# A transformer block with attention and expert layers: softmax probabilities normalised before their transposes, values as the stationary operand

## The chip, the cores and the metric

The kernel runs on one core of a Trainium2 chip. The metric is the device time of one execution in microseconds; three runs of the kernel before gave 843.80, 843.96 and 844.66 (median 843.96). A core has a matrix engine (TensorE, PE in the profile; its weight loads are PEld), VectorE (DVE), ScalarE (ACT), GpSimd (POOL) and a queue for DMA issues (SyncE, SP). Each works through its own list in order, and they meet at semaphores.

## The reference

`x` is 64 sequences of 750 rows of 128. Three layers follow one another:

```
h   = conv_patches(x) @ W + b           # patches of 16 rows, stride 8: 93 tokens of 128 per sequence
h  += attention(layernorm(h))           # 8 heads of 64; q, k, v each: 128x512 product, then a causal 3-tap filter
      sim  = q k^T * 64^-0.5 - slope_h * |i - j|, masked above the diagonal
      attn = softmax(sim, over j);  out = (attn v) @ wout^T
h  += expert_layer(layernorm(h))        # 16 experts, top 2; per expert the mean over its tokens of silu(x w1^T),
                                        # times w2, mixed by the two routing weights
```

## The kernel before

Sequences are taken in 16 groups of four. The program is written out by hand as a software pipeline over t = 0 to 20 (`run`, `step(t, u, f)` on each engine), and each t has four steps s = 0 to 3, one sequence in each. In step (t, s) an engine does in a fixed order, as far as the stage flags `f` allow: token products of group t (`f.tok`), the first normalisation and its transposes of group t-1 (`f.norm`), the query, key and value products of group t-2 (`f.proj`, three of twelve blocks in a step, each with its tap filter: `tap2` on ScalarE and `conv` on VectorE), attention of sequence n = 4(t-3)+s (`f.attn`), the second normalisation, gating and ranks of group t-4 (`f.gate`), and the scatter of group t-5's rows to the experts' rows in HBM (`f.scat`). t = 6 to 13 run as a hardware loop. A "full group" below is a t in which all stages are on, or all but the scatter.

Attention of one sequence (93 tokens) crosses two steps. In its own step: the scores into the two banks `psS` (a bias product with the identity in bf16, L516, then 8 head products of depth 64, L521), on VectorE the row maximum (L876) and the subtraction into `shifted` (L879). In the next step: 8 transposes of `shifted` back into `psS` (L452), on ScalarE the exponential into `probT` (L700, two halves), then 8 products into `psO` with `probT[:, h]`, 93 keys by 93 queries, as the stationary operand and the values with a column of ones, 93 by 65, moving (L500). Queries then lie on partitions; column 65 of each head is the softmax denominator. VectorE takes its reciprocal (L867) and multiplies (L870) into `attn`, TensorE turns it back by four transposes (L544), ScalarE copies them to `attnT` (L746), and the output projection follows (L576), which VectorE adds to `resid` (L891). The values themselves come by four transposes (L469) and a copy to `vrow` (L710).

Single buffers set much of the order: `psS` serves scores, then transposed probabilities; `psV` serves the value transposes, the transposes of the result and those of the routing weights; `psO` serves the weighting, the output projection (`psWout`), `psHn`, the gate and the ranks. The split products (L406 to L408) are fp32 products in three fp32r parts; their low parts are made by GpSimd (`low`, L1043, and L1096).

GpSimd's list in a step: the small operations of the normalisations (s = 1 and 2), `low` for the next step's token products, `xnT_lo` (s = 3), two indirect scatters (L1106), which wait in s = 0 for the slots that VectorE's `place` writes. From t = 17 on, when `f.norm` is off, all eight scatters of a group are issued at the head of s = 0. VectorE's list begins step s = 0 with `place` (L931), s = 1 and s = 2 with statistics, s = 3 with `choose`; `route` ends s = 2. On ScalarE `normalise` (L684) comes before `tap2` of block 3s+1 in s = 1 and s = 2.

After t = 20 come tables, the expert tiles (L595 to L617, L768 to L794, L995 to L1015), the second expert layer (L633 to L642) and the mix. The change doesn't touch them.

Of the kernel before, what the change touches and what calls it, by code (L numbers as in the profile page):

```python
# [27 lines left out]
ALU = mybir.AluOpType  # L28
# [29 lines left out]
def build(nc, x, w_tok, b_tok, gamma, beta, wq, wk, wv, cq, ck, cv, w_out, w_gate, w1, w2,  # L58
# [3 lines left out]
    with ctx:  # L62
# [41 lines left out]
        vrow = [sb(f"vrow{u}", [NT, H, DH + 1]) for u in range(2)]  # L104
        rmax = sb("rmax", [NT, 2, 4])
        shifted = sb("shifted", [NT, 2, 4, NT])
        probT = sb("probT", [NT, 2, 4, NT])
        rden = sb("rden", [NT, 2, 4])
        attn = sb("attn", [NT, H * DH])
# [50 lines left out]
        with ExitStack() as phase1:  # L160
# [24 lines left out]
        psTot = psO[:, 0, 264:264 + E]  # L185
# [20 lines left out]
        consts_ready, zeros_ready, taps_ready, bias_cast, vones_ready, rwzero_ready = (  # L206
            sem("consts_ready"), sem("zeros_ready"), sem("taps_ready"), sem("bias_cast"),
            sem("vones_ready"), sem("rwzero_ready"))
# [11 lines left out]
        p_tr, p_evac, pv_mm, den_done, norm_done = (  # L220
            sem("p_tr"), sem("p_evac"), sem("pv_mm"), sem("den_done"), sem("norm_done"))
        a_tr, a_evac, out_mm, res_add = sem("a_tr"), sem("a_evac"), sem("out_mm"), sem("res_add")
# [180 lines left out]
        def _(pe):  # L403
# [38 lines left out]

            def step(t, u, f):
                for s in range(GB):
                    n = (t - 3) * GB + s
                    prev = f.attn and s > 0 or f.last and s == 0
                    if prev:

                        pe.wait_ge(shift_done, n)
                        for a in range(2):  # L450
                            for hh in range(4):
                                mm = nc.tensor.transpose(psS[:NT, a, hh * NT:(hh + 1) * NT], shifted[:, a, hh, :],  # L452
                                                         ident[:NT, :NT])
                            mm.then_inc(p_tr, 1)
                    if f.gate and s == 2:
                        wait(pe, hn_ready, t - 3)
                        wait(pe, norm_done, n - 1 if f.attn else B)
                        for b in range(GB):
                            mm = nc.tensor.transpose(psHn[:, b * NT:(b + 1) * NT], hn[u][:, b, :],
                                                     ident[:NT, :NT])  # L460
                        mm.then_inc(hnT_tr, 1)
                    if f.proj and s == 0:
                        proj(t, u, f, 3 * s)
                    if f.attn:
                        if s == 0:
                            pe.wait_ge(conv_done, (t - 2) * NBLK)
                        wait(pe, a_evac, n - 1)
                        for j in range(QB):
                            mm = nc.tensor.transpose(psV[:NT, j * 128:(j + 1) * 128],  # L469
                                                     qkv[1 - u][:, 2 * QB + j, s, :], ident[:, :])  # L470
                        mm.then_inc(v_tr, 1)
                    if f.proj and s > 0:
                        proj(t, u, f, 3 * s)
# [10 lines left out]
                    if f.tok:  # L484
                        tok_taps(t, s, 0, 1)
                    if prev:

                        pe.wait_ge(p_evac, n * 2)
                        pe.wait_ge(v_evac, n)
                        wait(pe, norm_done, n - 1)  # L490

                        wait(pe, res_add, n - 1)
                        if f.gate and s == 2:
                            wait(pe, hnT_evac, t - 3)
                        if f.gate and s == 3:
                            wait(pe, logit_copy, t - 3)
                        if f.scat and s == 0:
                            wait(pe, pos_done, t - 4)
                        for h in range(H):
                            mm = nc.tensor.matmul(psO[:NT, h // 4, (h % 4) * (DH + 1):(h % 4 + 1) * (DH + 1)],  # L500
                                                  probT[:, h % 2, h // 2, :], vrow[(s + 1) % 2][:, h, :],
                                                  start=True, stop=True)
                        mm.then_inc(pv_mm, 1)
# [6 lines left out]
                    if f.attn:  # L510

                        if s == 0 and isinstance(t, int) and t == 3:
                            pe.wait_ge(bias_cast, 4)
                        wait(pe, p_evac, n * 2)
                        for a in range(2):
                            nc.tensor.matmul(psS[:NT, a, 0:4 * NT], ident16[:NT, :NT], bias[:, a, :],  # L516
                                             start=True, stop=False, skip_group_check=True)
                        for hh in range(4):
                            for a in range(2):
                                lo = 64 * a  # L520
                                mm = nc.tensor.matmul(psS[:NT, a, hh * NT:(hh + 1) * NT],  # L521
                                                      qkv[1 - u][lo:lo + 64, hh, s, :], qkv[1 - u][lo:lo + 64, QB + hh, s, :],
                                                      start=False, stop=True, skip_group_check=True)
                        mm.then_inc(s_mm, 1)

                    if f.proj:
                        proj(t, u, f, 3 * s + 1)
                    if f.tok:
                        tok_taps(t, s, 1, 2)
                    if f.attn and prev:  # L530
                        pe.wait_ge(v_evac, n + 1)
                    if f.scat and s == 0:

                        wait(pe, rw_done, t - 4)
                        wait(pe, a_evac, n - 1 if prev else B)
                        mm = nc.tensor.transpose(psRT, rw[:, :, :].rearrange("p b e -> p (b e)"),
                                                 ident[:NT, :NT])
                        if not prev:
                            mm.then_inc(rwT_tr, 1)
                    if prev:  # L540

                        pe.wait_ge(norm_done, n)
                        for j in range(QB):
                            mm = nc.tensor.transpose(psV[:, j * NT:(j + 1) * NT], attn[:, j * 128:(j + 1) * 128],  # L544
                                                     ident[:NT, :NT])
                        mm.then_inc(a_tr, 1)
# [24 lines left out]
                    if prev:  # L571
                        pe.wait_ge(a_evac, n)
                        if f.gate and s == 3:
                            wait(pe, base_done, t - 3)
# [85 lines left out]
        def _(ac):  # L660
# [31 lines left out]
            def step(t, u, f):  # L692
                for s in range(GB):
                    n = (t - 3) * GB + s
                    prev = f.attn and s > 0 or f.last and s == 0
                    if prev:
                        wait(ac, pv_mm, n - 1)
                        for a in range(2):
                            ac.wait_ge(p_tr, n * 2 - 1 + a)
                            nc.scalar.activation(probT[:, a, :, :].rearrange("p h n -> p (h n)"),  # L700
                                                 psS[:NT, a, 0:4 * NT], ACT.Exp).then_inc(p_evac, 1)
# [471 lines left out]
```

## Time and profile before

| | |
|---|---|
| runs | 843.80, 843.96, 844.66 us |
| profiled execution: time, span | 846.1 us, 844.4 us |
| busy, share of the span | PE 89%, PEld 82%, DVE 73%, ACT 56%, POOL 45% |
| granted TensorE clock, mean | 0.943 |
| first and last bias product (L516) | 78.9 and 651.4 us |

The span runs from the first instruction to the last; the execution's time holds 1.7 us around it. A row of the timeline gives start, length, engine, line, operation, output and inputs; where products of one line follow one another, they are merged and the last column counts them. An fp32 product counts as two matmul instructions, a split product's parts (fp32r) and a transpose as one each. Products overlap in their records, so the time that one takes from the next is read from start to start. In the groups by line the numbers behind the first bar are the busy time in us and the mean of one in ns, behind the second the engine's idle time just before them, with what ended it.

### The profile page before, as it was taken

The page shows a single profiled execution, that of the slowest core. Times are in us where ns is not written, and L with a number is a line of the kernel's source. Part 1 is how long each engine was busy: PE and PEld are TensorE (multiplying, and loading weights), DVE is VectorE, ACT ScalarE, POOL GpSimd, SP SyncE. Part 2 cuts the span into 40 slices and gives each one's busy share as a digit, 9 for nine tenths or more (in the row PEclk, how much of TensorE's full clock was granted, in tenths as well). Part 3 has the DMA queues.
Part 4 walks back from the last instruction along what each step waited for, and adds up shares of the span by engine and source line. Part 5 has one row for each costly group of instructions (what it writes and reads, how often), then busy time and mean ns, then how long its engine had stood idle before and what let it go on. Part 6 is the DMA issues. An engine that isn't in the chain of part 4 may idle for free. (4 is left out here: it accounts for less than half of the span.)

```text
span 844.4 us, 20971 instructions
## 1 busy us (share of the span) xinstructions
PE 752.6 (89%) x6670; PEld 696.4 (82%) x6670; DVE 615.9 (73%) x1621; ACT 468.9 (56%) x1021; POOL 383.3 (45%) x408
## 2 busy tenths in 40 slices
PE   5577999999999999999999999999786318999987
PEld 5466999999999999999999999977675208999983
DVE  2145778888888888888888888899573145888865
ACT  3345566656566665656666566555333107899950
POOL 3442243666556565555656556545241552222200
PEclk9787999999999999999999999999898658999989
DMA  6321123332112112111212211050000022222205
GB/s 190 99 72 46 47 72 117 102 104 64 48 47 66 47 47 65 50 46 46 68 46 50 65 48 48 19 208 20 10 15 6 19 69 73 64 62 62 62 17 145
DMA packets 42246, 53.89 MB, mean 64 GB/s; under 512 B 13651, under 2 KB 28947, under 8 KB 41680
## 3 DMA queue, kind: packets, MB, share of 16 engines
q1 hardware_dynamic: 26304, 37.13, 15.5%
q0 software_dynamic: 13120, 14.05, 6.0%
q10 hardware_dynamic: 2768, 2.00, 0.8%
q8 instruction: 32, 0.52, 0.3%
q14 instruction: 22, 0.18, 0.1%
HBM read 42.69 MB, written 10.26 MB: 63 GB/s over the span
## 5 line engine op out<-in xcount | busy, mean ns | idle before, releaser
L1106 POOL DMA_INDIRECT expert_rows<-hn,slot x128 | 167.7, 1310 | 92.5 <-DVE slot L951 59.9
L1043 POOL TENSOR_TENSOR x_lo<-x_raw,x_hi 128x752 fp32r<-128x752 f32 x64 | 114.9, 1795 | 151.7 <-ACT x_hi L667 151.7
L831 DVE SCALAR_TENSOR_TENSOR qkv<-ps,taps,qkv 128x368 f32<-128x368 f32 x192 | 114.0, 594 | 86.2 <-ACT qkv L675 84.6
L675 ACT ACTIVATE qkv<-ps,taps 128x372 f32<-128x372 f32 x192 | 108.6, 567 | 90.1 <-PE ps L408 89.8
L834 DVE SCALAR_TENSOR_TENSOR qkv<-ps,taps,qkv 128x364 f32<-128x364 f32 x192 | 114.6, 597 | 6.8
L406 PE MATMUL ps<-x_hi,wtok_hi 128*128 128x376 f32 x256 | 95.3, 372 | 11.3 <-DVE wtok_lo L811 9.0
L500 PEld LDWEIGHTS psO<-vrow,probT 93*93 93x93 f32 x1024 | 93.5, 162 | 4.7 <-ACT probT L700 3.2
L500 PE MATMUL psO<-vrow,probT 93*93 93x65 f32 x1024 | 93.9, 245 | 2.0 <-ACT probT L700 1.1
L407 PE MATMUL ps<-x_lo,wtok_hi 128*128 128x376 f32 x256 | 89.1, 348 | 0.0
L408 PE MATMUL ps<-x_hi,wtok_lo 128*128 128x376 f32 x256 | 89.0, 348 | 0.0
L576 PE MATMUL psO<-wout,attnT 128*93 128x128 f32 x512 | 70.6, 283 | 18.6 <-ACT attnT L746 15.8
L998 DVE TENSOR_REDUCE qkv<-qkv 128x512 f32 (+1 forms) x108 | 72.3, 681 | 19.1 <-ACT qkv L771 18.6
L406 PE MATMUL ps<-xnT_hi,wqkv_hi 128*128 128x372 f32 x192 | 78.0, 406 | 9.0 <-DVE qkv L834 5.0
L576 PEld LDWEIGHTS psO<-wout,attnT 128*93 128x93 f32 x512 | 63.8, 167 | 22.4 <-ACT attnT L746 19.8
L700 ACT ACTIVATE probT<-psS 93x372 f32<-93x372 f32 x128 | 54.4, 472 | 47.9 <-PE psS L452 47.6
L312 POOL DMA_DIRECT2D xs<-expert_rows x54 | 29.8, 552 | 82.2 <-PE psS L595 41.3
L407 PE MATMUL ps<-xnT_lo,wqkv_hi 128*128 128x372 f32 x192 | 65.0, 339 | 0.0
L408 PE MATMUL ps<-xnT_hi,wqkv_lo 128*128 128x372 f32 x192 | 65.0, 338 | 0.0
L876 DVE TENSOR_REDUCE rmax<-psS 93x8 f32<-93x744 f32 x64 | 59.2, 926 | 7.0 <-PE psS L521 5.9
L667 ACT ACTIVATE x_hi<-x_raw 128x752 fp32r<-128x752 f32 x64 | 52.7, 823 | 19.1 <-DMA x_raw<-in_x 14.4
L879 DVE TENSOR_TENSOR shifted<-psS,rmax 93x744 f32<-93x744 f32 x64 | 59.4, 929 | 5.2
L521 PEld LDWEIGHTS psS<-qkv 64*93 64x93 f32 x1024 | 47.2, 158 | 18.2 <-issue 18.2
(160 smaller groups left out, 1620.7 us busy)
## 6 DMA issues: line engine op xcount, KB each, us to landing
x_raw<-in_x SPq DMA_DIRECT2D x64, 376.0 KB, 3.2
w1s<-in_w POOLq DMA_DIRECT2D x8, 512.0 KB, 4.9
w<-in_w SPq DMA_DIRECT2D x4, 1024.0 KB, 10.3
xs<-expert_rows SPq DMA_DIRECT2D x54, 64.0 KB, 1.8
xs<-expert_rows POOLq DMA_DIRECT2D x54, 64.0 KB, 2.1
out<-resid SPq DMA_DIRECT2D x16, 160.0 KB, 2.4
expert_rows<-hn,slot POOLq DMA_INDIRECT x128, 3.5
qkv<-in_w_tok ACTq DMA_DIRECT2D x4, 256.0 KB, 6.7
```

What stands on the lines that cost most here:

```text
L406: nc.tensor.matmul(dst, w_hi, x_hi, start=start, stop=False)
L407: nc.tensor.matmul(dst, w_hi, x_lo, start=False, stop=False)
L408: return nc.tensor.matmul(dst, w_lo, x_hi, start=False, stop=stop)
L500: mm = nc.tensor.matmul(psO[:NT, h // 4, (h % 4) * (DH + 1):(h % 4 + 1) * (DH + 1)], probT[:, h % 2, h // 2, :], vrow[(s + 1) % 2][:, h, : ...
L576: mm = nc.tensor.matmul(psWout, attnT[:, j, :], wout[:, j, :], start=(j == 0), stop=(j == QB - 1))
L675: nc.scalar.activation(qkv[u][:, k, :, :], psP[(k + 1) % 2][:, 0:GT].rearrange("p (b n) -> p b n", n=NT), ACT.Copy, scale=taps[:, k, 2:3]) ...
L831: nc.vector.scalar_tensor_tensor(dst[:, :, 1:NT], src[:, :, 0:NT - 1], taps[:, k, 1:2], dst[:, :, 1:NT], ALU.mult, ALU.add).then_inc(tap1_ ...
L834: nc.vector.scalar_tensor_tensor(dst[:, :, 2:NT], src[:, :, 0:NT - 2], taps[:, k, 0:1], dst[:, :, 2:NT], ALU.mult, ALU.add).then_inc(conv_ ...
L879: nc.vector.tensor_tensor(shifted[:, :, :, :], heads(psS, NT), rmax[:, :, :].unsqueeze(3).broadcast_to([NT, 2, 4, NT]), ALU.subtract).then ...
L998: nc.vector.tensor_reduce(part[:, bass.ds(i, 1), :].rearrange("p i j -> p (i j)"), act[k][:, :].rearrange("p (j n) -> p j n", n=128), AXX, ...
L1043: nc.gpsimd.tensor_tensor(x_lo[u][:, 0:PIECE], x_raw[u][:, :], x_hi[u][:, 0:PIECE].bitcast(F32), ALU.subtract)\
L1106: nc.gpsimd.indirect_dma_start(rows, bass.IndirectOffsetOnAxis(slot[1 - u][:, c:c + 1], 0), hn[1 - u][:, c % GB, :], None)\
```

## The change

- The subtraction writes to one of two new buffers `prob` (queries on partitions). ScalarE takes the exponential there, in place, in the same step; VectorE sums each head's row and takes the reciprocal; GpSimd multiplies in place. The transposes then turn finished probabilities, and ScalarE's two copies after them are plain copies.
- `vrow` loses its column of ones. In `weigh` the values (93 by 64) are stationary and `probT` moves (93 by 93); heads alternate between output partitions 0 to 63 and 64 to 127, so that `psO` holds the result already transposed. `attn`, its product, its four transposes and their semaphores go.
- Each engine's order in a step is written anew: the scores open the step on TensorE, the probabilities' transposes come after half of the token products and wait for the current sequence's subtraction; on VectorE maximum and subtraction open the step, and `place` follows the reciprocal; on ScalarE x_hi comes first and `normalise` last.

```diff
+            def scores(t, u, s, n):
+                if s == 0:
+                    wait(pe, conv_done, (t - 3) * NBLK + 2 * QB)
...
+                wait(pe, shift_done, n)
+                wait(pe, p_evac, (n - 1) * 2)
...                                                  (bias and head products as before)
+            def values(t, u, f, s, n):
+                if s == 0:
+                    pe.wait_ge(conv_done, (t - 2) * NBLK)
+                wait(pe, v_evac, n)
+                if f.scat and s == 1:
+                    wait(pe, rwT_evac, t - 4)
...                                                  (four transposes as before)
+            def turn_prob(f, s, n):
+                pe.wait_ge(prob_ready, n)
+                if f.attn:
+                    pe.wait_ge(shift_done, n + 1)
+                for a in range(2):
+                    for hh in range(4):
+                        mm = nc.tensor.transpose(psS[:NT, a, hh * NT:(hh + 1) * NT], prob[(s + 1) % 2][:, a, hh, :],
+                                                 ident[:NT, :NT])
+                    mm.then_inc(p_tr, 1)
+            def weigh(s, n):
+                pe.wait_ge(p_evac, n * 2)
+                pe.wait_ge(v_evac, n)
+                wait(pe, a_evac, n - 1)
+                wait(pe, res_add, n - 1)
+                for hh in range(4):
+                    for a in range(2):
+                        mm = nc.tensor.matmul(psO[64 * a:64 * a + 64, 0, hh * NT:(hh + 1) * NT],
+                                              vrow[(s + 1) % 2][:, 2 * hh + a, :], probT[:, a, hh, :],
+                                              start=True, stop=True)
+                mm.then_inc(pv_mm, 1)
```

The order on TensorE in a step after the change: `scores`, `proj` 3s, `values`, transposes of tokT (s = 0) or xn (s = 3), token taps 0 and 1, `turn_prob`, transposes of hn (s = 2), `proj` 3s+1, tap 2, transpose of rw (s = 0), `weigh`, gate (s = 2) or ranks (s = 3), tap 3, `proj` 3s+2, output projection.

```diff
@@ ScalarE, order in a step: high, tap2 3s, value copy, resid (s = 0), xnT and xnT_hi (s = 3), then
+                    if f.attn:
+                        ac.wait_ge(shift_done, n + 1)
+                        p = prob[s % 2][:, :, :, :].rearrange("p a h n -> p (a h n)")
+                        nc.scalar.activation(p, p, ACT.Exp).then_inc(exp_done, 1)
...                      the two copies to probT (ACT.Copy), hnT (s = 2), tap2 3s+1, rwT (s = 0), attnT from
...                      psO[:, 0, 0:GT] behind pv_mm, egap (s = 3), tap2 3s+2, normalise (s = 1, 2), tokT (s = 3)
@@ VectorE, order in a step: maximum, subtraction into prob, stats (s = 1, 2), choose (s = 3), conv 3s, then
+                    if f.attn:
+                        dve.wait_ge(exp_done, n + 1)
+                        wait(dve, prob_ready, n)
+                        nc.vector.tensor_reduce(den[:, :, :], prob[s % 2][:, :, :, :], AXX, ALU.add).then_inc(sum_done, 1)
+                        dve.wait_ge(sum_done, n + 1)
+                        nc.vector.reciprocal(rden[:, :, :], den[:, :, :]).then_inc(rden_done, 1)
+                    if f.scat and s == 0:
+                        place(t - 5, 1 - u)
...                      conv 3s+1, rank (s = 3), conv 3s+2, residual addition, route (s = 2)
@@ GpSimd, after xnT_lo and before the two scatters of the step
+                    if f.attn:
+                        pool.wait_ge(rden_done, n + 1)
+                        p = prob[s % 2][:, :, :, :]
+                        nc.gpsimd.tensor_tensor(p, p, rden[:, :, :].unsqueeze(3).broadcast_to([NT, 2, 4, NT]), ALU.mult)\
+                            .then_inc(prob_ready, 1)
```

## Rows read from the trace of the kernel before

**Rows 1.** Busy time by stage; columns in order: stage, length, PE, PEld, DVE, ACT, POOL, clock, DMA, GB/s.
```profile
78.91:112.82 33.91, 33.91 (x314) 32.06 (x313) 26.40 (x51) 20.89 (x42) 9.65 (x9) 1.00 0.17 47
112.82:551.76 438.94, 438.94 (x4139) 415.24 (x4139) 372.25 (x1044) 267.09 (x562) 253.82 (x252) 1.00 0.22 62
551.76:583.73 31.97, 29.38 (x296) 25.39 (x295) 29.91 (x87) 18.01 (x41) 14.17 (x18) 1.00 0.30 110
583.73:623.99 40.26, 32.66 (x289) 28.83 (x289) 29.22 (x79) 15.56 (x34) 12.91 (x13) 0.87 0.05 11
623.99:693.90 69.91, 31.45 (x289) 26.43 (x288) 28.96 (x117) 13.66 (x33) 33.14 (x32) 0.71 0.13 32
```

**Rows 2.** TensorE in order of time, within one step of a full group (start, length).
```profile
303.31 1.46 PE L500 MATMUL psO<-vrow,probT 93*93 93x65 f32 x16
304.61 0.48 PE L516 MATMUL psS<-bias,ident 93*93 93x372 bf16 x2
305.02 0.90 PE L521 MATMUL psS<-qkv 64*93 64x93 f32 x16
305.85 0.44 PE L406 MATMUL ps<-xnT_hi,wqkv_hi 128*128 128x372 f32 x1
306.13 0.33 PE L407 MATMUL ps<-xnT_lo,wqkv_hi 128*128 128x372 f32 x1
306.30 0.33 PE L408 MATMUL ps<-xnT_hi,wqkv_lo 128*128 128x372 f32 x1
307.49 0.48 PE L544 MATMUL psV<-ident,attn 93*128 93x93 f32 x4
307.76 0.41 PE L406 MATMUL ps<-x_hi,wtok_hi 128*128 128x376 f32 x1
308.01 0.34 PE L407 MATMUL ps<-x_lo,wtok_hi 128*128 128x376 f32 x1
308.88 1.04 PE L576 MATMUL psO<-wout,attnT 128*93 128x128 f32 x8
```

**Rows 3.** TensorE in order of time, the expert phase's second layer.
```profile
819.26 5.92 PE L639 MATMUL ps<-w,mean 128*32 128x128 f32 x128 [0.36 <-DVE mean L1021]
```

**Rows 4.** Groups by line and shape, whole span (busy us, mean ns, idle before).
```profile
L1043 POOL TENSOR_TENSOR x_lo<-x_raw,x_hi 128x752 fp32r<-128x752 f32 x64 | 114.9, 1795 | 151.7 <-ACT x_hi L667 151.7
L1096 POOL TENSOR_TENSOR xnT_lo<-xnT,xnT_hi 128x372 fp32r<-128x372 f32 x16 | 15.8, 985 | 10.6 <-ACT xnT_hi L726 10.6
L876 DVE TENSOR_REDUCE rmax<-psS 93x8 f32<-93x744 f32 x64 | 59.2, 926 | 7.0 <-PE psS L521 5.9
L879 DVE TENSOR_TENSOR shifted<-psS,rmax 93x744 f32<-93x744 f32 x64 | 59.4, 929 | 5.2
L870 DVE TENSOR_TENSOR attn<-psO,rden 93x512 f32<-93x512 f32 x64 | 43.9, 686 | 3.1 <-DVE rden L867 0.2
L867 DVE RECIPROCAL rden<-psO 93x8 f32<-93x8 f32 x64 | 12.7, 198 | 8.8 <-PE psO L500 8.8
L667 ACT ACTIVATE x_hi<-x_raw 128x752 fp32r<-128x752 f32 x64 | 52.7, 823 | 19.1 <-DMA x_raw<-in_x 14.4 <-PE ps L408 4.7
L675 ACT ACTIVATE qkv<-ps,taps 128x372 f32<-128x372 f32 x192 | 108.6, 567 | 90.1 <-PE ps L408 89.8
L710 ACT ACTIVATE vrow<-psV 93x512 f32<-93x512 f32 x64 | 38.2, 597 | 10.3 <-PE psV L469 10.3
L723 ACT ACTIVATE xnT<-ps,bet,gam 128x372 f32<-128x372 f32 x16 | 10.6, 661 | 23.7 <-PE ps L508 23.7
L726 ACT ACTIVATE xnT_hi<-xnT 128x372 fp32r<-128x372 f32 x16 | 8.2, 513 | 0.5
L700 ACT ACTIVATE probT<-psS 93x372 f32<-93x372 f32 x128 | 54.4, 472 | 47.9 <-PE psS L452 47.6
```

**Rows 5.** GpSimd in order of time, around one late train of scatters.
```profile
622.64 1.37 POOL L1106 DMA_INDIRECT expert_rows<-hn,slot  x1 [24.99 <-DVE slot L951]
635.21 0.19 POOL L1077 TENSOR_SCALAR veps<-mv 93x4 f32<-93x4 f32 x1
```

More of the change, by code:

```diff
@@ L446, in step @@
                     prev = f.attn and s > 0 or f.last and s == 0
[L447 to L462, printed above, removed]
+                    if f.attn:
+                        scores(t, u, s, n)
+                    if f.proj:
                         proj(t, u, f, 3 * s)
                     if f.attn:
[L465 to L473, printed above, removed]
+                        values(t, u, f, s, n)
                     if f.norm and s == 0:
@@ L483, in step @@
                         mm.then_inc(tok_tr, 1)
[L484 to L503, printed above, removed]
                     if f.norm and s == 3:
@@ L509, in step @@
                         mm.then_inc(xnT_tr, 1)
[L510 to L524, printed above, removed]
+                    if f.tok:
+                        tok_taps(t, s, 0, 2)
+                    if prev:
+                        turn_prob(f, s, n)
+                    if f.gate and s == 2:
+                        wait(pe, hn_ready, t - 3)
+                        wait(pe, base_done, t - 4)
+                        for b in range(GB):
+                            mm = nc.tensor.transpose(psHn[:, b * NT:(b + 1) * NT], hn[u][:, b, :],
+                                                     ident[:NT, :NT])
+                        mm.then_inc(hnT_tr, 1)
                     if f.proj:
@@ L572, in step @@
                         pe.wait_ge(a_evac, n)
-                        if f.gate and s == 3:
-                            wait(pe, base_done, t - 3)
                         for j in range(QB):
@@ L695, in step @@
                     prev = f.attn and s > 0 or f.last and s == 0
[L696 to L701, printed above, removed]
-                    if f.gate and s == 2:
-                        wait(ac, hnT_tr, t - 3)
-                        nc.scalar.activation(hnT[:, :], psHn, ACT.Copy).then_inc(hnT_evac, 1)
+                    if f.tok and f.more(t, s):
+                        ac.wait_ge(x_in[(s + 1) % 2], t * (16 * GB // 2) + (16 * ((s + 1) // 2) + 16))
+                        high(t * GB + (s + 1), (s + 1) % 2)
+                    if f.proj:
+                        tap2(t, u, 3 * s)
                     if f.attn:
@@ L752, in step @@
                         tap2(t, u, 3 * s + 2)
+                    if f.norm and s == 2:
+                        normalise(t - 1, rstd, shift, xn, ln_shift, xn_ready)
+                    if f.gate and s == 1:
+                        wait(ac, scattered[u], (t - u - 4) * (16 * GB))
+                        normalise(t - 4, rstd2, shift2, hn[u], ln2_shift, hn_ready)
                     if isinstance(t, int) and t == 0 and s == GB - 1:
@@ L800, in _ @@
         def _(dve):
-            for u in range(2):
-                nc.vector.memset(vrow[u][:, :, DH:DH + 1], 1.0).then_inc(vones_ready, 1)
             nc.vector.memset(zeros[:, :], 0.0).then_inc(zeros_ready, 1)
```

129 lines of the change are left out of this document (60 added, 69 removed).

## The prediction

> **What bounds the kernel now.** I read the page first (busy shares and the forty slices), then cut the span at the first bias product (L516) of a group of four sequences and asked for busy time by stage, then laid out one step's instructions, then the groups by line, then the drain. The reader is to see three things. From 112.8 to 551.8 us, which is twelve groups of four steps, TensorE is busy for all of the 438.9 us, so a group takes 438.94/12 = 36.58 us and nothing but TensorE's own instruction stream sets it; VectorE is busy 372.3 of them (31.0 a group), ScalarE 267.1 (22.3) and GpSimd 253.8 (21.2) [rows 1]. The group before (78.9 to 112.8) is the same kind, so 13 groups are TensorE's. In the next group, without token products, VectorE carries 29.9 of 32.0 us [rows 1]. In the last three groups of attention and gating (583.7 to 693.9) TensorE is busy for little more than half: these are chains of waits, and there the order of operations counts. The expert phase (150.5 us) isn't touched.
>
> **The change on TensorE, full groups.** Removed per step: the weighting with probabilities stationary, from 303.31 to the next line's start at 304.61, 1.30 us; and the four transposes of the normalised result, 307.49 to 307.76, 0.27, after which the first split product takes 0.25 instead of 0.17 to hand over (307.76 to 308.01, against 306.13 to 306.30): 0.35 in all [rows 2]. Added: the weighting with values stationary, 16 instructions of 93 columns that alternate between the lower and the upper 64 output partitions. Nearest row from below: the scores, also 16 instructions of 93 columns in pairs, on two halves of the rows; they take 305.02 to 305.85, 0.83, and cost 0.11 more at the next product (305.85 to 306.13 against 0.17) [rows 2]. That parts of the columns also run side by side is borne out at L639: 128 instructions of 128 columns on four column quarters take 5.92 us [rows 3], where the output projection takes 1.04 us for 8 of that width [rows 2], a pace at which 128 would need 16 us. So eight slots, 0.83 + 0.11, and about 0.10 for entering, which sits in the 0.41 us from the bias products to the first score: 1.03 us (an estimate; ends 0.66, eight slots of 0.083 and no edge, and 1.60, sixteen in a row with both edges). Moving the probability transposes between split products adds one more hand-over, 0.05 to 0.08. Net per step: -1.30 - 0.35 + 1.03 + 0.05 = -0.57, so 36.58 - 2.28 = 34.3 a group.
>
> The Trainium skill ("TensorEngine Tiling (Array Packing)", section "Key Properties") says that a change of tiling mode drains TensorE. By that the kernel now pays twice per step where it paid once; the two edges of the scores (0.11 behind them) are what the trace shows of it. If the drain were free, a step would be 0.2 cheaper than in my sum.
>
> **What is late next.** All other engines get a new chain: scores, row maximum, subtraction, then in the same step the transposes of the probabilities of the sequence before reuse the scores' banks, so they wait for this subtraction. On VectorE that is 0.93 + 0.93 [rows 4] from the scores' end and three hand-overs, 2.1 us (an estimate); TensorE has three projection products, four value transposes and six token products to do meanwhile: 9 x 0.17 [rows 2] + about 0.4 and the edges, 2.1. A tie in steps 1 and 2, with 0.3 to 0.4 to spare in 0 and 3. Any lateness of VectorE now stalls TensorE at once, where before it had a whole half step to spare.
> VectorE's load: the product with the reciprocal (0.69) goes, a sum over 744 elements (by the maximum's row, 0.93) comes, the reciprocal stays [rows 4]: 31.0 + 4 x 0.24 = 32.0 a group, or 32.6 with gaps between; below 34.3, but step 2 alone (statistics and routing) holds about 9.4 against TensorE's 9.
> ScalarE: step 3 starts with the normalisation of step 2 still running (moved to the end of its step), then x_hi 0.82, scaling 0.57, values 0.60, xnT 0.66 and its high part 0.51 come ahead of the exponential (about 0.8, by x_hi's width) and of the two copies (2 x 0.47) [rows 4]. Sum from the scores' end about 5 us; TensorE wants the copies after about 4.2. A stall near 0.5 once a group.
> GpSimd: four products of 744 elements, each about 1.78 by the 752-element row (1.80) [rows 4]: 21.2 + 7.1 = 28.3 busy, and 0.3 of idle issue behind each of 8 scatters, with gaps 33. That fits under 34.3 with little to spare; the product is due only in the next step, so it is covered. Its broadcast operand isn't in the trace; bounds 0.99 (the 372-element row, L1096) and 2.8 (that row on top of L1043's 1.80) [rows 4]; I take the row of like width.
> Of the possible 0.3 to 1 us of stalls I take 0.5, so 34.8 a group: 13 x (36.58 - 34.8) = -23 us.
>
> **The stages behind.** In the group from 551.8 VectorE is nearly full already and gains 1.0 of work: +0.8. In the groups of 583.7 and 624.0 GpSimd issues eight scatters in one train, released by the slots that `place` writes: at 622.64, until its next work at 635.21, 12.6 us [rows 5]; four small operations and ScalarE's normalisation follow, and TensorE waits for it. `place` moves from the head of step 0 behind scores (1.2), maximum and subtraction (2.0), exponential (0.8), sum and reciprocal (1.1): the train starts 5.1 us later. And the product of sequence 0 now stands behind the train in GpSimd's order, and before it those small operations: 1.8 more, on the path to TensorE's transposes, copies and weighting. Walking both groups through their waits gives +7.3 for the second (no projections in it) and +4.1 for the first, where projections and their additions had filled the time anyhow. The group after that has no attention and keeps its train; the start, before 78.9, gets a few reordered ScalarE operations: 0, bounds -1 and +2.
>
> Sum: -23.4 + 0.8 + 4.1 + 7.3 = -11.2. Against the profiled execution's 846.1 us that is 834.9; the median of the runs is 2.1 below that execution, so **832.5 us**.
>
> **Rivals.**
> *The drain and the edges cost nothing (0.15).* Weighting at 0.66 and no stalls: TensorE 33.0 and VectorE 32.6 a group bound alike, about 33.3: 13 x 3.3 = -43, with +12 behind: 813. For it: the eight-slot rhythm of the scores; against it: the 0.11 edge and the tie at the subtraction.
> *VectorE is held by GpSimd (0.15).* `place` sits right behind the reciprocal that releases GpSimd's product. If VectorE's first two-operand instruction there has to wait until that product ends (1.8 [rows 4]), step 0 takes VectorE 9.6 against TensorE's 8.5; the next step's subtraction comes 1.0 to 1.6 late in every group that scatters: +11 to +18 us, 844 to 850, the gain gone. In the trace no such pair has met, so no row tells for or against. The Trainium skill has this as a rule ("SBUF — State Buffer", section "SBUF: two separate sides": an exclusive lock for a whole instruction, between GpSimd and a VectorE operation with two SBUF inputs); this is the rule that speaks against the change.
> *GpSimd becomes the bound (0.08), slower than before.* Place: its in-order stream of casts, products and scatters. From a product of about 2.2 us on (33 + 4 x 0.45 = 34.8) it sets the group; at its upper bound of 2.8 the group is 33 + 4 x 1.0 = 37.0: 13 x 0.4 = +5, with +12 behind: 861. At 2.5, near 848.
> *Column halves don't run side by side (0.05).* Sixteen in a row, 1.60: 0 net per step, stalls 0.2: 36.8 a group, +3, and +12: 859. Against it stands L639.
> *The drain of the pipeline costs twice my walk (0.07):* +24 instead of +12: 845.
> The forecast itself, 818 to 843, has 0.50.
>
> **Numbers.** About 0.2% (1.7 us) is what a measurement of this kernel can tell from no change. Faster: forecast and first rival, 0.65 and a little of the others, 0.68. Same: the lower edge of VectorE's case and of the long drain, 0.07. Slower 0.25. The range takes the first rival's value and VectorE's case whole, and leaves out serial columns and a slow GpSimd: 812 to 853.
>
> **What would show it.** Right: the bias products 34.5 to 35 us apart per group, the weighting's 16 instructions within 0.85 us, TensorE's waits short and on the subtraction or the copies, the first scatter of the last groups 5 us deeper in its step. Wrong: the weighting at 1.3 us or more; GpSimd's product over 2.3 us or GpSimd busy for over 95% of a group; VectorE's `sel` lengthened or late beside a GpSimd product; TensorE idle for 1 us per step.

## The result, and the profile after

The changed kernel takes **899.22 us** (median of 4 runs, 891.68 to 903.10); the kernel before takes 843.88 (842.54 to 844.66) on the same chip. The ratio is 1.0647, with a 95% interval of 1.0574 to 1.0719: **slower**. The forecast was 832.5 us with a range of 812 to 853, so it was wrong in sign and in size. The profiled execution took 900.48 us, with a span of 898.7.

Busy time by stage, cut at the bias product of a group (now L452), with the columns of [rows 1]: the group of t = 3 (nothing to gate yet), twelve full groups, the group without token products (t = 16), the group of t = 17, and the rest up to the last train of scatters. Then two single steps, both a step 0.

```profile
66.83:98.26 31.43, 30.61 (x278) 27.06 (x277) 27.16 (x52) 22.60 (x43) 15.38 (x13) 1.00 0.19 55
98.26:575.88 477.62, 434.75 (x3950) 380.67 (x3949) 406.03 (x1037) 302.38 (x611) 318.94 (x297) 0.96 0.20 55
575.88:615.90 40.02, 32.05 (x284) 27.20 (x283) 33.76 (x89) 22.30 (x47) 21.48 (x22) 0.86 0.31 115
615.90:663.61 47.71, 34.16 (x275) 28.83 (x273) 30.46 (x80) 19.34 (x39) 19.06 (x18) 0.79 0.05 11
663.61:736.67 73.06, 40.02 (x292) 32.77 (x290) 24.48 (x103) 17.09 (x37) 29.59 (x29) 0.57 0.05 12
334.68:347.94 13.26, 10.50 (x82) 9.04 (x81) 10.39 (x24) 6.81 (x13) 9.38 (x7) 0.89 0.16 41
375.15:386.88 11.73, 9.04 (x83) 7.64 (x82) 9.48 (x23) 6.19 (x13) 8.81 (x7) 1.00 0.18 43
```

The reader is to see that a full group takes 477.62/12 = 39.80 us instead of 36.58, that TensorE now stands still for 42.9 us of the twelve groups where it had stood still for none, and that its clock there is no longer 1.00. Added up against [rows 1]: the first bias product comes 12.1 us earlier (66.83 against 78.91), these 13 groups cost 36.2 more (509.05 against 472.85), the group behind them 8.1 more, the next 7.4, and what follows up to the last train of scatters (736.67 against 681.18) 15.9. That makes 55.5; what follows, most of it the expert phase, gives 1.2 back.

From bias product to bias product the four steps of a full group took 8.7, 8.9, 9.55 and 9.5 us. Now they take 11.7 to 13.5, 8.1, 9.1 and 9.85 in most groups. Over the twelve full groups step 0 costs 45.7 us more, step 3 costs 7.3 more, and steps 1 and 2 cost 8.3 and 6.0 less, which is near the forecast. So **nearly all of the loss is in step 0**. Step 0 in order of time (start, length, engine, idle before and its releaser):

```profile
381.10 0.20 DVE L869 RECIPROCAL rden<-den 93x8 f32<-93x8 f32 x1
381.22 0.11 DVE L924 TENSOR_SCALAR wden<-egap 93x4 f32<-93x4 f32 x1
381.38 1.43 POOL L1092 TENSOR_TENSOR prob<-prob,rden 93x744 f32<-93x744 f32 x1 [0.41 <-DVE rden L869]
381.46 1.49 DVE L928 TENSOR_TENSOR sel<-hot,pos 93x128 f32<-93x128 f32 x1
...
383.50 0.22 DVE L944 TENSOR_TENSOR rw<-wsel 93x64 f32<-93x64 f32 x1
...
383.78 0.30 PE L543 MATMUL psV<-ident,rw 93*128 93x93 f32 x1 [2.68 <-DVE rw L944]
384.08 0.87 PE L493 MATMUL psO<-probT,vrow 93*64 93x93 f32 x16
```

TensorE's stream now has the transpose of the routing weights (L543) ahead of the weighting. It waits for `rw`, the last product of `place`, and `place` has gone behind the sum and the reciprocal. The waits of TensorE over ten full groups that scatter (total us, times, longest):

```profile
PE psV L543 <- DVE rw L944: 27.3, 10, 2.9
PE psS L481 <- DVE prob L851: 9.9, 10, 1.0
```

Once per group TensorE waits 2.7 us for `rw`, and once, in step 3, 1.0 us for the subtraction. Within the first wait stands `sel` at 1.49 us; where no GpSimd work runs beside it, it takes 0.26. The second wait comes from `route` at the end of step 2: it holds VectorE from 366.59 to 368.24, and the row maximum of step 3, whose scores ended at 366.62, begins only behind it:

```profile
366.59 0.21 DVE L888 COPY logit<-psO 93x64 f32<-93x64 f32 x1
...
368.10 0.14 DVE L897 TENSOR_TENSOR gap<-top 93x4 f32<-93x4 f32 x1
368.16 0.92 DVE L848 TENSOR_REDUCE rmax<-psS 93x8 f32<-93x744 f32 x1
...
370.19 0.90 PE L481 MATMUL psS<-ident,prob 93*93 93x93 f32 x8 [1.03 <-DVE prob L851]
```

The groups of the new instructions, and `sel` (busy us, mean ns, idle before):

```profile
L1092 POOL TENSOR_TENSOR prob<-prob,rden 93x744 f32<-93x744 f32 x64 | 91.3, 1427 | 88.0 <-DVE rden L869 87.9
L867 DVE TENSOR_REDUCE den<-prob 93x8 f32<-93x744 f32 x64 | 58.6, 915 | 11.5 <-POOL prob L1092 8.9 <-ACT prob L719 2.6
L719 ACT ACTIVATE prob<-prob 93x744 f32<-93x744 f32 x64 | 52.7, 823 | 22.4 <-DVE prob L851 22.4
L928 DVE TENSOR_TENSOR sel<-hot,pos 93x128 f32<-93x128 f32 x16 | 18.7, 1170 | 0.0
```

The weighting in a step 2, which answers to the first line of [rows 2]: its 16 products are through at the next line's start, after 0.79 us.

```profile
361.84 0.87 PE L493 MATMUL psO<-probT,vrow 93*64 93x93 f32 x16
362.63 0.83 PE L551 MATMUL psO<-wgate,hnT 128*93 128x16 f32 x8
```

The clock. Of the two step 0 above one takes 13.26 us and one 11.73 with nearly the same instructions. In the longer one the wait ends at 343.42, TensorE runs on at 0.98 until 345.0, and from there the granted clock is 0.50, the 1.2 GHz level. The clock fell to 0.50 within 2 us of the end of this wait in 8 of the 11 full groups that scatter. The row:

```profile
345.00:346.50 1.50, 1.50 (x7) 1.47 (x6) 0.00 (x0) 0.14 (x2) 1.20 (x2) 0.50 0.09 12
```

In the late groups GpSimd's order is what [rows 5] showed, with the product in it:

```profile
634.78 1.28 POOL L1102 DMA_INDIRECT expert_rows<-hn,slot  x1 [0.30 <-issue]
636.09 1.44 POOL L1092 TENSOR_TENSOR prob<-prob,rden 93x744 f32<-93x744 f32 x1
637.62 0.19 POOL L1068 TENSOR_SCALAR veps<-mv 93x4 f32<-93x4 f32 x1
```
```profile
637.58 1.56 PE L481 MATMUL psS<-ident,prob 93*93 93x93 f32 x8 [7.46 <-POOL prob L1092]
```

The product of sequence 0 stands behind a train of eight scatters (623.64 to 636.06), and TensorE waits 7.46 us for it.

### The profile page after: what moved, and what is told of

Read it like the earlier page. It is cut to its first block and busy times, and to the rows that moved or that the text cites. A ratio compares the mean times of both kernels' runs of the same rounds, so it can differ in the third digit from the quotient of the medians.

```text
span 898.7 us, 20634 instructions
## 1 busy us (share of the span) xinstructions
PE 752.1 (84%) x6414; PEld 659.8 (73%) x6414; DVE 656.0 (73%) x1619; ACT 516.6 (57%) x1085; POOL 475.2 (53%) x472
## 5 line engine op out<-in xcount | busy, mean ns | idle before, releaser
L1092 POOL TENSOR_TENSOR prob<-prob,rden 93x744 f32<-93x744 f32 x64 | 91.3, 1427 | 88.0 <-DVE rden L869 87.9
L406 PE MATMUL ps<-x_hi,wtok_hi 128*128 128x376 f32 x256 | 99.8, 390 | 9.5 <-DVE wtok_lo L805 8.6
L481 PE MATMUL psS<-ident,prob 93*93 93x93 f32 x512 | 58.8, 261 | 40.4 <-DVE prob L851 26.5
L481 PEld LDWEIGHTS psS<-ident,prob 93*93 93x93 f32 x512 | 49.6, 168 | 54.9 <-issue 23.7
L574 PE MATMUL psO<-wout,attnT 128*93 128x128 f32 x512 | 81.7, 313 | 1.8 <-ACT attnT L737 1.7
L574 PEld LDWEIGHTS psO<-wout,attnT 128*93 128x93 f32 x512 | 76.3, 192 | 3.9 <-ACT attnT L737 2.8
L867 DVE TENSOR_REDUCE den<-prob 93x8 f32<-93x744 f32 x64 | 58.6, 915 | 11.5 <-POOL prob L1092 8.9
L457 PEld LDWEIGHTS psS<-qkv 64*93 64x93 f32 x1024 | 51.1, 170 | 21.3 <-issue 21.3
L719 ACT ACTIVATE prob<-prob 93x744 f32<-93x744 f32 x64 | 52.7, 823 | 22.4 <-DVE prob L851 22.4
```

The costliest lines, as they stand in the source:

```text
L406: nc.tensor.matmul(dst, w_hi, x_hi, start=start, stop=False)
L574: mm = nc.tensor.matmul(psWout, attnT[:, j, :], wout[:, j, :], start=(j == 0), stop=(j == QB - 1))
L1092: nc.gpsimd.tensor_tensor(p, p, rden[:, :, :].unsqueeze(3).broadcast_to([NT, 2, 4, NT]), ALU.mult)\
```

## Experiments

Ratios are to the kernel before on the same chip. Unless said otherwise a kernel is the changed one with the edit shown. "Full groups" are measured from bias product to bias product, "the drain" from the last transposes of tokens (L481 before, L515 after) to the start of the last train of scatters, that of t = 20 (131.2 us before, 158.5 after). They are read from the one profiled execution of each kernel; the times are medians of all.

**1. The transpose of the routing weights late in its step.** On TensorE, behind the output projection; ScalarE's copy `rwT` behind the last tap filter. The edit in short:

```diff
 (TensorE, step 0, ahead of `weigh`)
-    wait(pe, rw_done, t - 4); nc.tensor.transpose(psRT, rw, ...)
 (TensorE, step 0, behind the output projection)
+    wait(pe, rw_done, t - 4); nc.tensor.transpose(psRT, rw, ...)
```


> The changed kernel with one thing moved: TensorE's transpose of the routing weights (which waits for VectorE's place) goes from ahead of the weighting to the end of step 0, and ScalarE's copy of it behind the last tap scaling. Theory A (the loss in full groups is this wait, 2.7 us, and the TensorE clock that falls after it): step 0 of a full group goes from 13.3 to about 9.0 us, the group from 40.2 to 36.0, granted clock 1.00 from 147 us on; the whole 845 to 855 us. Theory B (VectorE is the bound, held by GpSimd's products through the shared port, and TensorE's wait only shows it): step 0 stays at 11.5 or more because place still ends at the same time and the next step's subtraction comes late; 880 us or more.

Measured: 857.84 us (856.93 to 858.68), ratio 1.0162 (1.0136 to 1.0188). That is 3 us above theory A's range and far from theory B's 880. The wait is gone, step 0 is 8.9 us, most full groups are 36.6 to 36.9, and TensorE's clock there is 1.00. Taking this one wait out, with its clock loss, brought back **41 of the 55 us**. `sel` still takes 1.5 us, and now it costs something one step later: VectorE ends the list of step 0 late, so step 1's subtraction is late, and TensorE waits 0.7 to 1.0 us for it. Step 1 takes 9.0 us where it was 8.1:

```profile
294.03 0.90 PE L481 MATMUL psS<-ident,prob 93*93 93x93 f32 x8 [0.73 <-DVE prob L851]
```

**2. `place` back at the head of VectorE's step 0.**

```diff
+    if f.scat and s == 0: place(t - 5, 1 - u)     # ahead of the row maximum
...
-    if f.scat and s == 0: place(t - 5, 1 - u)     # behind the reciprocal
```


> The changed kernel with place back at the head of VectorE's step 0, as in the kernel before; the transpose stays ahead of the weighting. Theory A: the wait for the routing weights goes too, but row maximum and subtraction come 1.2 us later in step 0, less 0.4 of slack: step 0 about 9.8 us, group 36.8; and the trains of eight scatters in the last groups start 5 us earlier in their step, so the drain gets shorter by some 8 to 10 us: about 850 us in all, near or a little below the other variant. Theory B (port): place no longer meets GpSimd's product, so sel falls from 1.47 to 0.26 us and the same 850 would follow; the two theories part on the other variant. If the drain's loss was not from place, the drain stays as long as now (158 us from the last transpose of tokT to the last scatter train).

Measured: 898.98 us (895.4 to 899.08), ratio 1.0646 (1.062 to 1.0673): a miss. `place` no longer meets the product, it meets a scatter's issue and GpSimd's low part of x:

```profile
259.43 1.29 POOL L1102 DMA_INDIRECT expert_rows<-hn,slot  x1 [0.30 <-issue]
...
259.91 2.64 DVE L941 CAST slot<-slotf 93x8 int32<-93x8 f32 x1
260.74 1.78 POOL L1033 TENSOR_TENSOR x_lo<-x_raw,x_hi 128x752 fp32r<-128x752 f32 x1
...
264.64 1.26 PE L481 MATMUL psS<-ident,prob 93*93 93x93 f32 x8 [3.84 <-DVE prob L853]
```

A cast of 8 columns takes 2.64 us (0.16 elsewhere) and ends with `x_lo`; the row maximum and the subtraction are late, and TensorE waits 3.84 us. Step 0 takes 14.2. The drain is 16.6 us shorter, as expected.

**3. No product on GpSimd.** The probabilities are not normalised; TensorE waits for the reciprocal instead.

```diff
-    nc.gpsimd.tensor_tensor(p, p, rden[...].broadcast_to(...), ALU.mult).then_inc(prob_ready, 1)
-    pe.wait_ge(prob_ready, n)
+    pe.wait_ge(rden_done, n)
```


> GpSimd's product is left out, so the probabilities are not normalised and the output is not the reference's; TensorE's transposes wait for the reciprocal in its place. Theory A: the 2.7 us wait in step 0 shrinks by sel's 1.2 us only, and with it part of the clock loss: step 0 about 10.5 to 12, group 37.5 to 39, and 1.4 us shorter per late group; about 875 us. Theory B (GpSimd's product is the cause): the group falls to 36 and the whole to 850 or less.

Measured: 885.87 us (884.96 to 886.78), ratio 1.0491 (1.0455 to 1.0527). Neither number. Step 0 falls to 9.9 to 10.1 in most groups, but GpSimd, now earlier, runs `x_lo` beside another small instruction, ahead of step 3's row maximum. TensorE's wait for the subtraction grows from 1.0 to 2.4 us, and step 3 takes 12.7 to 14.3, part of it at the lower clock:

```profile
289.17 1.81 POOL L1032 TENSOR_TENSOR x_lo<-x_raw,x_hi 128x752 fp32r<-128x752 f32 x1
...
289.45 1.56 DVE L896 TENSOR_TENSOR gap<-top 93x4 f32<-93x4 f32 x1
```

`gap` subtracts 4 columns; alone it takes 0.14. So the hold is not a matter of the new product.

**4. The weighting one column half after the other**, so that neighbours share output partitions.

```diff
-    for hh in range(4):
-        for a in range(2):
+    for a in range(2):
+        for hh in range(4):
```


> The weighting takes all heads of the lower 64 output partitions first, then those of the upper, so that neighbouring products share a column half. If the halves ran side by side before, the 16 instructions take about 1.3 us in place of 0.8, 0.5 more per step, 64 steps: +30 us, about 930. If they did not, no change from 899.

Measured: 975.81 us (975.29 to 976.33), ratio 1.1556 (1.1518 to 1.1594), 46 us above the 930 expected. Until the next line's start the weighting takes 1.17 us in steps 1 and 2, where it took 0.79, and step 2 grows by 0.37 (9.08 to 9.45):

```profile
302.25 1.24 PE L493 MATMUL psO<-probT,vrow 93*64 93x93 f32 x16
303.42 0.83 PE L551 MATMUL psO<-wgate,hnT 128*93 128x16 f32 x8
```

So with alternating halves neighbours do overlap, for 0.38 us of 1.17. Most of the rest is the hold again: the shift puts `gap` beside a scatter and `x_lo` (2.50 us at 356.60), and step 3 takes 16.7, part of it at the lower clock.

**5. The routing weights' transpose in a bank of its own.** Experiment 1, and the transpose writes to `psO`; `place` behind the second `conv` pair.

```diff
-    psRT = psV[:, 384:384 + NT]
+    psRT = psO[:, 1, 128:128 + NT]
```


> On top of the late transpose of the routing weights: its PSUM target moves from the values' bank to the free bank of psO, so that the next step's value transposes no longer wait for ScalarE's copy, and place goes behind the filter of block 3s+1, so that sel no longer starts under GpSimd's product. Theory A (what is left are single waits): step 1 falls from 9.0 to 8.1, sel from 1.47 to 0.26 us, group 36.8 to 35.9; about 848 us. Theory B (VectorE or GpSimd is the bound by load): group stays at 36.5 or more.

Measured: 848.16 us (846.07 to 849.54), ratio 1.0044 (1.0025 to 1.0063): the time is as expected, but one reason was wrong. Full groups are 36.1, and step 1 is back at 8.1. The expectation gave this to the bank. In experiment 1 no wait of TensorE for the copy of the routing weights stands in the trace, only those for the subtraction, so it comes from `place`: `sel` is at 257 ns in all 16 groups, since `place` now lies where GpSimd doesn't multiply. No run has one of the two edits alone.

**6. VectorE's routing out of the way of the subtraction.** Experiment 5, and `route` leaves the end of step 2 and goes behind the subtraction of step 3; `choose` and `rank` move back to make room. The ranks' products go to the end of TensorE's step, and ScalarE's `egap` behind its last tap filter.

```diff
@@ VectorE, behind the subtraction
                     if f.gate and s == 3:
-                        choose(t - 4)
+                        route(t - 4)
...
@@ VectorE, behind conv of block 3s+1
                     if f.gate and s == 3:
-                        rank(t - 4, u)
+                        choose(t - 4)
...
@@ VectorE, end of the step
-                    if f.gate and s == 2:
-                        route(t - 4)
+                    if f.gate and s == 3:
+                        rank(t - 4, u)
```


> In addition routing moves from the end of step 2 behind the subtraction of step 3, choose behind the filter of block 3s+1, the ranks on TensorE and VectorE to the end of step 3, so that VectorE is free when step 3's scores end and its small operations miss GpSimd's casts. Theory A: step 3 falls from 9.85 to about 9.0 (ScalarE's list keeps about 0.4 of stall), group about 35.1; 838 us. Theory B (ScalarE's normalisation at the head of step 3 is the cause of the 9.85): no change against the kernel without this move.

Measured: 837.49 us (835.5 to 838.8), ratio 0.9912 (0.9883 to 0.9942), as expected. Most full groups take 35.3 to 35.6.

**7. Experiment 6, with the scatters of t = 17, 18 and 19 spread over their steps**, two in each; only t = 20 keeps its train.

```diff
-    if f.scat and not f.norm and s == 0:     # eight in one train
+    if f.scat and not f.gate and s == 0:
...
-    if f.scat and f.norm:                    # two per step
+    if f.scat and f.gate:
```


> In addition the scatters of the last groups are issued two per step instead of eight at the head of step 0, except in the very last. If the train on GpSimd, with the products queued behind it, is what makes the late groups long, the groups of t = 17 and 18 fall from 47 and 38 to about 36 and 32 and the drain is 15 to 20 us shorter: about 820 us. If those groups are long by their chain of waits anyhow, the gain is under 5 us.

Measured: **810.02 us** (807.2 to 813.59), ratio **0.9592** (0.9551 to 0.9633), below the 820 expected. The group of t = 17 takes 33.2 us where it took 45.1 in experiment 6, and the drain is 122.3 where it was 148.1.

**8. The kernel before, with that edit of the scatters alone.**

> The kernel before with only the spread scatters. Its late groups hold no products on GpSimd, the train delays only the second normalisation: 40.3 falls to about 34 and 35 to about 28 for t = 17 and 18, and the group behind gains 6: about 826 us, which then is what the changed kernel has to beat.

Measured: 827.55 us (826.68 to 828.13), ratio 0.98 (0.9776 to 0.9825), as expected. So this edit, which has nothing to do with the change, wins 17 us on the kernel before.

**9. The kernel before, with an idle GpSimd product per step** that nobody waits for.

```diff
+    nc.gpsimd.tensor_tensor(idle, idle, idle8[...].broadcast_to(...), ALU.mult)
```


> The kernel before with one more GpSimd product per step (93 x 744, in place, on a tile that nobody reads), at the place in GpSimd's list where the changed kernel has its own; nobody waits for it. If VectorE and GpSimd share a port exclusively, VectorE instructions with two SBUF operands or a cast between SBUF tiles that start beside it take 1 us or more in place of 0.15 to 0.29; those with a PSUM operand keep their length. TensorE has half a step of spare there, so the time grows by 0 to 6 us, most of it in the late groups, where the product stands behind the train (2 x 1.4 us and more). If there is no such lock, no VectorE instruction gets longer.

Measured: 848.81 us (845.99 to 854.88), ratio 1.0068 (1.0039 to 1.0097). Full groups stay at 36.6 us; in the profiled execution, the slowest of ten at 854.88 us, the drain takes 142.9 where it was 131.2. In the full groups GpSimd can carry the product beside everything else. It settles little of the hold: the idle product met almost no small VectorE instruction (`sel` 256 ns, `hot` 288); one `wden` of 4 columns, begun ahead of it beside a scatter's issue, took 1.75 us.

**10. Experiment 7 without the product**; the probabilities are not normalised (edit as in 3).

> The reordered kernel with spread scatters, without GpSimd's product (probabilities not normalised, so the output is not the reference's). If the product is now off the path and seldom meets VectorE's small operations, the full groups stay at 35.3 to 35.6 and the whole at 805 to 810 us; if it still holds VectorE, groups fall to about 34.5 and the whole to under 800.

Measured: 803.9 us (802.6 to 805.2), ratio 0.9519 (0.9475 to 0.9563), between the two expectations: the product costs 6 us in all. Most full groups are 0.3 shorter without it, and those of t = 5 and 6 are 1.8 and 1.6 shorter. In experiment 7 the product of t = 5 met `hot`, which took 1.40 us, and TensorE waited 1.76 for the mask made of it.

**11. The kernel before, with ScalarE's two normalisations at the end of their steps**, as the change has them.

```diff
-    (ahead of tap2(t, u, 3 * s + 1))
+    (behind tap2(t, u, 3 * s + 2))
     if f.norm and s == 2: normalise(t - 1, rstd, shift, xn, ln_shift, xn_ready)
     if f.gate and s == 1: normalise(t - 4, rstd2, shift2, hn[u], ln2_shift, hn_ready)
```


> The kernel before with one edit: ScalarE's two normalisations (steps 1 and 2) stand at the end of their step, as in the changed kernel, not ahead of the second tap filter. The changed kernel reaches its third group's token transposes 8.5 us earlier than the kernel before (69.4 against 77.9 us), and in the kernel before TensorE waits there for 3.30 us, at 66.84, for VectorE's conv behind that normalisation, then runs with 0.51 to 0.52 us per split product where it took 0.33. Theory A (the early start is this move alone): third tokens' transposes at 69 to 71 us, full groups unchanged at 36.6, time 835 to 837, ratio 0.990. Theory B (the early start comes from the new data path or TensorE's new order): 844, transposes at 77 to 78.

Measured: 848.39 us (845.49 to 854.35), ratio 1.0056 (1.0032 to 1.0081). The start is near theory A's: the third tokens' transposes come at 70.1 us (77.9 before, 69.4 in the changed kernel). The total is nobody's: the full groups cost 37.6 instead of 36.6, most of it because the second normalisation is now late for TensorE in step 1 (9.77 instead of 8.9):

```profile
233.26 0.54 PE L459 MATMUL psO<-ident,hn 93*128 93x93 f32 x4 [0.66 <-ACT hn L688]
```

In the changed kernel the same move costs nothing, where TensorE takes those rows only in step 2 (L532 at 360.37, with the step's start at 356.2).

**12. Experiment 11 with the scatters spread.**

> The kernel before with the two edits of order together: the normalisations at the end of their step, and the scatters of the late groups two per step. It is the fair partner of the mended changed kernel (810.0 us). Theory A (the start's gain is the move of the normalisation and adds to the spread scatters): 827.6 - 8 = 819 to 820, so the new data path is worth 9 to 10 us, about 1 us in each of 12 full groups less what it costs behind. Theory B (the gains overlap or the early start needs the new data path): 827, and the data path is worth 17.

Measured: 830.03 us (829.84 to 830.13), ratio 0.9838 (0.982 to 0.9855). Neither theory's number: it is 2.5 us slower than experiment 8. The start wins 5.6 us (70.5 against 76.0) and the drain 3.0, and the groups between lose 12.4, most of it in step 1. The best partner for experiment 7, the kernel before with only the first normalisation moved and the scatters spread, wasn't run. From 8 and the start's gain of 5.6 to 7.8 (experiments 12 and 11) it would be near 820 to 822 (an estimate), which leaves the new data path with its mended order 10 to 12 us ahead. That isn't shown by a run; shown are the 17.5 us to experiment 8.

## Why the prediction was wrong

**What failed: "place moves", priced at GpSimd and not at TensorE.** The prediction followed `place` to its slots and the scatters they release. It never followed `rw`, the other thing that `place` writes, although the transpose of `rw` stands in TensorE's order ahead of the weighting. Before, `place` ran at the head of step 0 and TensorE never waited for it. Behind scores, maximum, subtraction, exponential, sum and reciprocal it is 2.7 us late in every full group that scatters; the sum had nothing for it. The prediction had listed that very chain, for the drain. Experiment 1 shows the price: 41 us.

**The clock came with it.** [Rows 1] show 1.00 over the twelve groups, so the forecast priced waits at their length. After this wait the clock fell to 0.50 in 8 of 11 groups, which in one pair of steps took 1.5 us more (13.26 against 11.73).

**The rival "VectorE is held by GpSimd" was true, but put in one place only.** In the changed kernel and experiments 1 to 4, `sel` took 1.476 us on average in all 36 groups where the product ran beside it, and 0.257 in all 44 where it didn't. It wasn't `sel` alone: `hot` takes 1.02 beside the low part of xn (27 of 27; 0.29 alone), `gap` up to 3.39 (experiment 4), and casts of 8 columns up to 2.65 beside `x_lo` and the issue of a scatter. Instructions that read PSUM (maximum, subtraction, `conv`) and the sum over 744 columns kept their lengths within 0.02 us beside GpSimd's elementwise work, in all runs. The Trainium skill ("SBUF — State Buffer", section "SBUF: two separate sides") names VectorE operations with two SBUF inputs and those in a two-port mode; these runs agree for `sel`, `hot` and `gap`, which have two inputs. The casts have one, and no run shows in which mode they ran. The rival's own mechanism, a late subtraction in the next step, shows in experiment 1: 0.7 to 1.0 us late, where 1.0 to 1.6 was forecast. In the changed kernel the wait for `rw` lay in front of it.

The statement that "no such pair has met" in the trace of before was wrong too. One row of it was there to be read:

```profile
L811 DVE TENSOR_TENSOR wtok_lo<-qkv,wtok_hi 128x512 fp32r<-128x512 f32 x4 | 3.8, 992 | 5.5 <-ACT wtok_hi L682 5.5
```

Four equal instructions with a mean of 992 ns are one of 1.9 us, begun at 7.00 beside the `x_lo` of 6.60 to 8.36, and three of 0.68. The price of +11 to +18 us counted neither TensorE's wait for `rw` nor that any shift of a step can bring another small instruction beside GpSimd's `x_lo` (experiments 2, 3 and 4).

**TensorE's saving** was right. The weighting took 0.79 us and its after-edge, against 0.83 + 0.11; steps 1 and 2 came out at 8.07 and 9.08 (8.9 and 9.55 less 0.57 gives 8.3 and 9.0). Two groups of experiment 7 show the whole of it, length and then TensorE's busy time:

```profile
451.00:485.80 34.80, 34.38 (x332) 30.67 (x330) 31.66 (x88) 25.03 (x52) 27.43 (x26) 1.00 0.22 57
380.40:415.70 35.30, 34.56 (x330) 30.73 (x330) 31.44 (x87) 24.86 (x52) 27.14 (x26) 1.00 0.21 55
```

TensorE's own work is 34.4 to 34.6 a group, so the saving is 2.0 to 2.2, or 0.50 to 0.55 a step where 0.57 was forecast. The forecast's 34.8 with 0.5 us of stalls is the first of these groups, but only behind the mends of experiments 1, 5 and 6; most groups there take 35.3 to 35.6. The sum itself had two slips of 0.3 us: it took -23.4 for the -23.1 of its own product, and 834.9 less 2.1 is 832.8.

**VectorE, ScalarE and GpSimd.** VectorE was busy for 406.03/12 = 33.8 us a group, against 32.0 to 32.6; the difference is the hold (`sel` 1.2 a group, and in step 3 `idxf` 0.8 and `hot` 0.7). ScalarE's copies, priced at a stall of 0.5 in step 3, held TensorE nowhere in the full groups. The 1.03 us stall of step 3 was the subtraction, late behind `route` on VectorE. The prediction had seen that step 2 holds more work for VectorE than for TensorE, and yet gave step 3 some spare time. GpSimd's product took 1.43 us, against 1.78 taken and bounds of 0.99 and 2.8; "GpSimd becomes the bound" needed a product of 2.2 us, and GpSimd was busy for 67% of the twelve groups; "column halves don't run side by side" is refuted by the 0.79 us and experiment 4.

**The start** was put at 0, bounds -1 and +2. It gained 8.5 us at the third tokens' transposes (the bias product gains more, as it also stands earlier in its step): in the kernel before, ScalarE's first normalisation stands ahead of the second tap filter, waits there for GpSimd, and TensorE waits 3.30 us behind it and runs on at a lower clock. Experiment 11 shows that the move alone brings 7.8 in one pair of executions. The start varies between executions, though: the third tokens' transposes came at 76.0 to 77.9 us in three profiles with the old order, at 70.1 and 70.5 in experiments 11 and 12, and at 65.9 to 69.4 in the nine of the changed kernel and its variants. So the move is most of the gain, and what brings the rest stays open.

**The drain** was +12.2, and is +31.4 up to the last train. The group from 575.88 was given +0.8 and took +8.1; experiment 1 takes 4.1 of that back, so half was the wait for `rw` again. For the other two the mechanism was right (product behind the train, `place` late) and the sizes were not: +7.4 for +4.1, +10.7 for +7.3 up to the last bias product, and 5.2 behind it. The group of t = 17, 47.7 us long, takes 41.4 with `place` at the head (experiment 2) and 39.3 without the product (3), against 40.3 before, so either one removes most of its loss. The sizes of the others stay open. With spread scatters the drain of the changed kernel is 122.3 and that of the kernel before 114.0, and leaving the product out brings only 1.6 of that (experiment 10, 120.7); the rest isn't explained.

## What to carry to other kernels

When a block of instructions moves, list everything that it writes and follow each to its reader in the order of every engine; the reader that stands ahead of the bound engine's main work sets the price. In a group of few instructions, compute lengths one by one before saying that a trace holds no case of an effect: a mean far from that of its equals is a case. Judge a new data path only after its order has been mended, and give the old one the same mends: here the change as made costs 6.5%, mended and with spread scatters it is 4.1% faster, and about half of that comes from an edit that wins 17 us on the old kernel too (experiment 8).

## What the runs showed of the hardware

- VectorE instructions of 4 to 128 columns per row, 0.14 to 0.29 us long alone, took up to 3.4 us beside GpSimd's elementwise work or across a scatter's issue, and `sel` ended 0.1 us behind GpSimd's product (382.95 against 382.81). In experiment 2 the hold began during the issue of a scatter (259.43 to 260.72) and went on through `x_lo`.
- A GpSimd product of 744 elements with a broadcast operand on 93 partitions took 1.43 us, less than the 1.80 us of the subtraction of two full operands over 752 on 128 ([rows 4], L1043).
- An idle time of 2.3 to 2.9 us in a stream at full clock was followed by a granted clock of 0.50 in 8 of 11 groups and not in the other three, at the same place of the loop.
